# Three places instead of two for layer two's gate and up weights, down weights fetched tile by tile, in a two-layer attention and feed-forward kernel

## The reference, cut to what matters

```python
x = x + _L0_xattn_ref(_layernorm(x), ctx_512, ...)
x = x + _L0_ffn_ref(_layernorm(x), ...)      # a dense gelu part (512 to 2048 to 512) and 8 experts, top 2
x = x + _L1_xattn_ref(_layernorm(x), ctx_512, ctx_512, ...)
x = x + _L1_ffn_ref(_layernorm(x), ...)      # silu(x @ w_gate.T) * (x @ w_up.T), then @ w_down.T
```

## Time and profile before

| | |
|---|---|
| median of 3 runs | 1854.75 us (1850.45 to 1861.82) |
| profiled execution, its own time | 1854.27 us |
| span of the profiled execution | 1852.5 us |
| TensorE busy | 1693.0 us, 91% |
| VectorE busy | 1130.6 us, 61% |
| ScalarE busy | 810.7 us, 44% |
| mean granted TensorE clock | 0.966 |

### The profile page before, as it was taken

The page is one execution under the profiler, slowest core; times in us unless marked ns, Lnnn a source line. Parts: engine busy times, 40 slices in busy tenths (PEclk is TensorE's granted clock), DMA queues, the critical chain, the costliest instruction groups (busy, mean ns, idle before and its releaser), DMA issues.

```text
span 1852.5 us, 27428 instructions
## 1 busy us (share of the span) xinstructions
PE 1693.0 (91%) x9460; PEld 1347.2 (73%) x9460; DVE 1130.6 (61%) x2444; ACT 810.7 (44%) x1799; POOL 267.1 (14%) x301
## 2 busy tenths in 40 slices
PE   3688997999989999888999999889999999999998
PEld 2566776878988887676766766677776678678887
DVE  5777679755665646974677764499556663543222
ACT  3566553234665643322565665323155461422111
POOL 1213234610121203220010100132100000000000
PEclk8689998999999999999999999999999999999999
DMA  3324548798888787879889863687862445245562
GB/s 104 114 92 165 182 164 292 245 358 281 262 284 327 248 289 287 308 258 340 298 261 302 283 221 112 233 292 272 301 208 89 120 137 205 80 144 196 195 215 92
DMA packets 135593, 410.06 MB, mean 221 GB/s; under 512 B 16032, under 2 KB 30752, under 8 KB 131744
## 3 DMA queue, kind: packets, MB, share of 16 engines
q1 hardware_dynamic: 123552, 368.98, 58.1%
q0 software_dynamic: 11904, 39.33, 6.5%
HBM read 303.92 MB, written 104.33 MB: 220 GB/s over the span
## 4 chain that ended last, share of the span: by engine, by line
PE 38%; DVE 5%; DMA 4%; ACT 2%; issue 2%; SPq 0%; ACTq 0%; DVEq 0%
PE ps L1226 10%; PE ps L1228 9%; PE ps L1227 9%; PE ps L1380 4%; PE ps L1389 2%; DMA gu<-w_dram 2%; PE ps L1372 2%; DMA raw<-in_ffn_w 1%; ACT Pr L1605 1%; PE ps L1373 1%; DMA w_dram<-raw 0%; DVE mnb L2008 0%; DVE raw L1737 0%; DVE x L2036 0%; PE ps L1232 0%
## 5 line engine op out<-in xcount | busy, mean ns | idle before, releaser
L1226 PE MATMUL ps<-xT,gu 128*128 128x512 f32 (+1 forms) x1392 | 531.2, 382 | 49.6 <-DMA gu<-w_dram 24.7
L1228 PE MATMUL ps<-xT,gu 128*128 128x512 f32 (+1 forms) x1392 | 512.6, 368 | 0.0
L1227 PE MATMUL ps<-xT,gu 128*128 128x512 f32 (+1 forms) x1392 | 512.2, 368 | 0.0
L1226 PEld LDWEIGHTS ps<-xT,gu 128*128 128x128 f32 x1392 | 269.9, 194 | 96.3 <-issue 46.1
L1228 PEld LDWEIGHTS ps<-xT,gu 128*128 128x128 f32 x1392 | 269.2, 193 | 43.1
L1227 PEld LDWEIGHTS ps<-xT,gu 128*128 128x128 f32 x1392 | 269.7, 194 | 35.5
L1226 PE MATMUL ps<-wd,hid 128*128 128x512 f32 x604 | 248.3, 411 | 28.9 <-issue 14.0
L1227 PE MATMUL ps<-wd,hid 128*128 128x512 f32 x604 | 238.0, 394 | 0.0
L1228 PE MATMUL ps<-wd,hid 128*128 128x512 f32 x604 | 237.9, 394 | 0.0
L1437 ACT ACTIVATE hid<-act 128x512 fp32r<-128x512 f32 (+1 forms) x174 | 99.9, 574 | 289.3 <-DVE act L1717 280.8
L1717 DVE TENSOR_TENSOR act<-act,ps 128x512 f32<-128x512 f32 (+1 forms) x174 | 106.7, 613 | 167.7 <-PE ps L1228 158.4
(11 more groups left out here) (283 smaller groups left out, 2362.4 us busy)
## 6 DMA issues: line engine op xcount, KB each, us to landing
gu<-w_dram SPq DMA_DIRECT2D x192, 512.0 KB
raw<-in_ffn_w SPq DMA_DIRECT2D x78, 768.0 KB
wd<-w_dram SPq DMA_DIRECT2D x96, 512.0 KB, 6.2
w_dram<-raw SPq DMA_DIRECT2D x48, 512.0 KB, 4.6
w_dram<-gu SPq DMA_DIRECT2D x16, 1024.0 KB, 10.2
raw<-in_ffn_w POOLq DMA_DIRECT2D x48, 256.0 KB, 5.3
QT<-q_dram SPq DMA_DIRECT2D x48, 256.0 KB, 5.9
y_dram<-x SPq DMA_DIRECT2D x23, 512.0 KB
```

Source lines behind the costliest of these rows:

```text
L1226: mm(out_ap, ah, bh, start=start, stop=False)
L1227: mm(out_ap, ah, bl, start=False, stop=False)
L1228: return mm(out_ap, al, bh, start=False, stop=stop)
```

## The change

It has three parts.

1. **A third place in layer two.** The space of `acc` is given back at once in the allocation, and a tile `gu_third` of the same size takes it. From the first tile of layer two on (`LAYER2`, s = 110) gate's and up's weights go round three places instead of two, and a load waits for tile s - 3 instead of s - 2. The first tile that uses the third place (F10.2) waits until `acc` of F03 has been stored (`dn_stored`).
2. **Down weights one tile at a time.** The plan holds each `("pre", s, 2)` behind `("pre", s, 1)` of the same tile. This holds in F02 and F03 too.
3. **Early pieces paced.** The plan holds `eload` n behind the start of tile F03.(n // 4), where before it held `eload` 0 alone behind the start of F03.0.

No arithmetic instruction and no byte moved is added or taken away.

```diff
+    LAYER2 = FIRST["F", 1, 0]
+    def gu_slot(s):
+        return (s - LAYER2) % 3 if s >= LAYER2 else s % 2
+    def gu_before(s):
+        return s - 3 if s > LAYER2 + 2 else s - 2 if s < LAYER2 + 2 else None
...
-            on = [("up" if m == 1 else "gate", s - 2)] if m < 2 else [("down", GROUP_OF[s - 6], group_tiles(GROUP_OF[s - 6]) - 1)] if s >= 6 else []
+            on = [("up" if m == 1 else "gate", gu_before(s))] if m < 2 and gu_before(s) is not None else [("dstore", LAST_DOWN["F", 0, 3], TB - 1)] if m < 2 else [("down", GROUP_OF[s - 6], group_tiles(GROUP_OF[s - 6]) - 1)] if s >= 6 else []
...
-        if item == ("eload", 0):
-            return [("gate0", FIRST["F", 0, 3])]
+        if item[0] == "eload":
+            return [("gate0", FIRST["F", 0, 3] + item[1] // 4)]
+        if item[0] == "pre" and item[2] == 2:
+            return [("pre", item[1], 1)]
...
-        acc = sb("acc", [P, TB, D])
+        acc_scope = ExitStack()
+        acc = sb("acc", [P, TB, D], F32, acc_scope)
+        acc_scope.close()
+        gu_third = sb("gu_third", [P, 2, 2, D], F32R)
...
+        def weights_at(s, m):
+            return gu_third[:, m, :, :] if gu_slot(s) == 2 else gu[:, gu_slot(s), m, :, :]
...
                     if m == 0:
-                        sp.wait_ge(gate_done, nth("gate", s - 2))
-                        load(gu[:, s % 2, 0, :, :].bitcast(F32), from_).then_inc(g_loaded[s % 2], 16)
+                        if gu_before(s) is None:
+                            sp.wait_ge(dn_stored, 16 * TB * B)
+                        else:
+                            sp.wait_ge(gate_done, nth("gate", gu_before(s)))
+                        load(weights_at(s, 0).bitcast(F32), from_).then_inc(g_loaded[gu_slot(s)], 16)
```

More of the change, by code:

```diff
@@ L608, in two_layers, with loads_of @@
             PIECE[item] = len(PIECE) + 1
[L610 to L615, removed]
+    def loads_of(tiles, place):
+        return {s: 16 * sum(1 for v in tiles[:n + 1] if place(v) == place(s)) for n, s in enumerate(tiles)}
+    GU_LOADS, WD_LOADS = loads_of(PRE, gu_slot), loads_of(PRE, lambda s: s % 6)
+    GU_STORES, WD_STORES = loads_of(KEPT, gu_slot), loads_of(KEPT, lambda s: s % 3)
     def early_store(n):
@@ L780, in two_layers @@
         w_high, w_low = sems("w_high", "w_low")
-        g_loaded, u_loaded, gu_stored = (sems(n + "0", n + "1") for n in ("gate_loaded", "up_loaded", "gu_stored"))
+        g_loaded, u_loaded = (sems(n + "0", n + "1", n + "2") for n in ("gate_loaded", "up_loaded"))
+        gu_stored = sems("gu_stored0", "gu_stored1")
         wd_loaded, wd_stored = sems(*(f"wd_loaded{n}" for n in range(6))), sems(*(f"wd_stored{n}" for n in range(3)))
@@ L960, in _ @@
                         if is_kept(s - 2):
-                            sp.wait_ge(gu_stored[s % 2], GU_STORES[s - 2])
+                            sp.wait_ge(gu_stored[gu_slot(s)], GU_STORES[s - 2])
                     else:
@@ L966, in _ @@
                     if m == 0:
-                        sp.wait_ge(gate_done, nth("gate", s - 2))
-                        load(gu[:, s % 2, 0, :, :].bitcast(F32), from_).then_inc(g_loaded[s % 2], 16)
-                    elif m == 1:
-                        sp.wait_ge(up_done, nth("up", s - 2))
-                        load(gu[:, s % 2, 1, :, :].bitcast(F32), from_).then_inc(u_loaded[s % 2], 16)
+                        if gu_before(s) is None:
[3 more added lines that the diff above has]
+                        load(weights_at(s, 0).bitcast(F32), from_).then_inc(g_loaded[gu_slot(s)], 16)
+                    elif m == 1:
+                        if gu_before(s) is None:
+                            sp.wait_ge(dn_stored, 16 * TB * B)
+                        else:
+                            sp.wait_ge(up_done, nth("up", gu_before(s)))
+                        load(weights_at(s, 1).bitcast(F32), from_).then_inc(u_loaded[gu_slot(s)], 16)
                     else:
@@ L1236, in quarter @@
                 q, cols = x_slot(s), columns(s)
-                return three(ps[:, gate_bank(s) + m, 0:width(s)], gu[:, s % 2, m, 0, rows(d)], gu[:, s % 2, m, 1, rows(d)],
+                return three(ps[:, gate_bank(s) + m, 0:width(s)], weights_at(s, m)[:, 0, rows(d)], weights_at(s, m)[:, 1, rows(d)],
                              xT[:, q, 0, d, cols], xT[:, q, 1, d, cols], d == 0, d == KD - 1)
@@ L1250, in _ @@
                     else:
-                        pe.wait_ge(g_loaded[s % 2], GU_LOADS[s])
+                        pe.wait_ge(g_loaded[gu_slot(s)], GU_LOADS[s])
                     if what == "E" and h == 0:
@@ L1271, in _ @@
                     else:
-                        pe.wait_ge(u_loaded[s % 2], GU_LOADS[s])
+                        pe.wait_ge(u_loaded[gu_slot(s)], GU_LOADS[s])
                     quarter(1, s, 0)
```

## The result

| | before | after |
|---|---|---|
| median | 1856.0 us of 4 runs (1850.45 to 1861.82) | 1828.03 us of 4 runs (1824.07 to 1835.68) |
| profiled execution, its own time | 1854.27 us | 1828.03 us |
| its span | 1852.5 us | 1826.3 us |

The ratio is 0.9854, with a 95% interval of 0.9809 to 0.9898: 28 us, or 1.5%, faster. The forecast was 1838 us, and the range of 1822 to 1859 holds the result.

The account below looks back on a forecast made before the run. TensorE, busy 1693.0 of 1852.5 us, sets the end; only its idle and low-clock time can be won. Terms 1.0 + 3.0 + 3.7 + 2.0 + 1.4 + 5.3 + 0.6 = 17.0 us, from 1854.75 to 1838; range 1822 to 1859.

Parts of the forecast that it names:

- the account that I held to be the likeliest: Whole kernel: waits for weights go, VectorE and the query loads take back half; 1830 to 1845 us, chance 0.43.
- a different placement of the same steps: Every order after F02.0 may shift in a new plan; worth about 6 us either way, taken as 0.
- F03.3, 3.0 us kept of 9.4: Layer one: down weights leave the queue's front, but full DMA returns the wait later; bounds 0 and 9.4 us, 3.0 kept.
- F10.8 and F10.11, 2.0 us kept of 11.9: Layer two: weight waits go, but VectorE, 91% busy, makes TensorE wait instead; bounds 0 and 11.9 us, 2.0 kept.
- The terms of the other tiles in the stretch: Third place's gains: 3.7 us at F10.7, 1.4 at F10.15, 5.3 of 5.9 at F11.3.
- F02, 1.0 us gain kept: F02's two waits for weights total 1.5 us; the down hold wins 1.0.
- 5.3 us at F11.3: Wait and slow stretch of 5.9 us; 5.3 kept because query loads follow the last step between the layers.
- Its price of 0 at F10.2: F10.2 must wait for the last store of `acc`; cost 1.4 us at most, taken as 0.
- The 10.4 us for low-clock stretches: After long weight waits TensorE ran at its lower clock; the stretches' losses sum to 10.4 us.
- B: All is won, VectorE steps spread over more tiles; up to 35.1 us, 1820 to 1830 us, chance 0.17.
- C: VectorE and DMA take nearly all, waits only change name; 7 us won, 1848 us (1845 to 1854.75), chance 0.25.
- D: F10.7 to F11.2: densely packed steps cost 10 us, slower than before; 1861 us (1855 to 1870), chance 0.15.

Follow-up runs that it names:

- e4: Kernel before plus the hold on down loads and the pace of early pieces, still two places: 1837.35 us, 0.9889.
- e2: Kernel before plus one down load at a time alone, two places everywhere: 1840.14 us, 0.9900.
- e10: Kernel before plus the down hold for F02 and F03 alone, layer two keeping its bursts and two places: 1838.12 us, 0.9914.
- e7: Changed kernel with the down hold only from F03 on, so F02 has its old order: 1844.43 us, 0.9915.
- e1: Changed kernel without the down hold and with the old hold on early pieces, leaving the third place alone: 1853.45 us, 0.9975.
- e6: Changed kernel with the steps between the layers for batches 2 and 3 held behind the start of F10.5: 1837.31 us, 0.9890.
- e8: Changed kernel with three places at run time from F10.6 on, but a plan made as if for two: 1836.71 us, 0.9872.
- e5: Changed kernel without the pace of the early pieces: 1829.16 us, 0.9851.
- e3: Kernel before plus the pace of the early pieces alone: 1854.43 us, 0.9982.
- e9: Kernel before plus the down hold for layer two's tiles alone, two places: 1861.62 us, 1.0038.

## Why the prediction was right, and where it was wrong

**What the whole is made of.** Both holds bring the time to 0.9889 (e4; 0.9900 as e2), nearly all of it by the hold in layer one (e10, 0.9914). The third place adds some 0.3%, the pace nothing. The forecast of 17.0 us had it the other way round: 13.0 us from the third place at F10.7 to F11.7, and 4.0 us from the down loads. That the range of 1822 to 1859 holds 1828 is in part luck: most of the gain came from a part that the sum had at 0, and the result lies outside the 1830 to 1845 of the account that I held to be the likeliest.

**The step that failed** is "So a different placement of the same steps is worth about 6 us either way. I take 0." The new plan was the largest term. e10 changes only the waits in the plan of layer one and moves the kernel by 16 us. I had bounded the value of a placement by one pair of waits in one stretch. F02 fits this bound (6.2 us dearer). But the order in F02 decides when the loads and steps of the next 350 us go out, and the bound says nothing of that.

**F03.3, 3.0 us kept of 9.4.** Undersized. The stretch F03.0 to F10.5 won 10.8 us, above even the upper end. I had reasoned that DMA, at a share of 1.03, would give the wait back at the first scores. With F02's old order that is what happened: e7 waits 6.65 us there for the queries. In the new order `KT` leaves 15.0 us earlier and the attention runs ahead of F03.3, so neither wait exists; a wait of 3.2 us for ScalarE inside the first scores is new. The reasoning held for the order that I looked at, not for the one that came. The wait itself is also unsteady: 7.2 us in the kernel before and 10.9 in e1, which has the same order up to there.

**F10.8 and F10.11, 2.0 us kept of 11.9.** Undersized, by the same cause. With the third place alone the mechanism is there: e1 waits 7.4 us for `hid` behind VectorE's list. But I took 93% for what VectorE manages, and it is at 94.9% from 1223 to 1287; and I held its list to begin where it had begun. It begins 18 us ahead of F10.5 now, and TensorE waits 5.4 us for `x` where it waited 4.7. e6 takes that start away and loses 9 us; as its rows show, the loss did not take the form of a longer wait for VectorE, so how much of the 20.2 us the early start explains is shown only to that 9. And e6 still wins 15.2 us in this stretch with the late start. The terms of the other tiles in the stretch (3.7, 1.4, 5.3) and the 11.9 sum to 22.3 us; 20.2 came.

**F02, 1.0 us gain kept.** Wrong in sign: 6.2 us dearer, with a 6.6 us wait for the copy into `acc`.

**The third place.** Right about what it does (waits for weights in its stretch 14.7 to 0, in e1 too) and about its size in its own stretch (12.7 measured in e1, 12.4 forecast). Wrong in that this stays: 8.3 us came back after F11.5. The prediction kept 5.3 us at F11.3 "because the attention of batches 2 and 3 follows, whose query loads come only after the last of those steps"; this is where it came back, with 4.4 us of waits for `QT`. Its price of 0 at F10.2 was right, though the margin was smaller: from the last store's issue to F10.2's first matmul 8.1 us (1135.5 to 1143.59), not 18.8, and the load itself had 5.6. The 20.2 us for store and load, each taken at 10.1, were far too high; the store landed in 2.4.

**The clock.** The 10.4 us for low-clock stretches were a fair size: in F10.5 to F11.5 TensorE's busy time fell by 6.4 us at 610 matmuls, of the 8.2 us counted there. Over the whole execution the mean granted clock did not rise, 0.966 before and 0.964 after.

**The pace.** Right: the same program.

**The rivals.** The result lies in the span that B had, by another way: B's VectorE work was to go later, and it went earlier. C's claim that waits only change their name is what e1 shows. D's claim, a dense plan that costs 6 us, came true in F02, at layer one's end, and in the next stretch the change won more than that. D's condition, a share of VectorE above 93% behind 1198, was met without its price.

**The signs.** Waits for weights under 5 us: yes, 2.7. Single down issues: mostly; one pair in F02 and one in F03, and from 1173.28 on one pair in each group of four. Two pairs of gate and up issues before a group's down products end: yes, but the kernel before has them too (1228.19 to 1236.37), so this sign tells nothing. VectorE above 93% with longer waits for `x`: 93.2 to 94.9%, waits 0.7 us longer. No wait before F10.2: yes. Loads of early pieces at the same tiles: no, the first three go out in F02.14 instead of F03.0; e2 has the same without the pace, so it is the order's doing. No wait for `QT` of over 5 us: yes. And "a gain or loss in stretches that had no `gu` wait, which would be the new plan's doing" was the sign that spoke: F02's loss.

**A rule weighed.** In 1173 to 1190 us DMA moved 398 GB/s at a share of 1.02, and TensorE was busy 17.00 of 17 us. The Trainium skill ("SBUF — State Buffer", section "A bandwidth-pool intuition that's wrong") gives about 358 GB/s from memory to a core, as its half of what two cores share. This trace is above that figure, as that of before was; the kernel runs on one core, and no run here loads a second. By my reading of the full share as "no more to be had", these 17 us would have cost time, and here they cost none. In the kernel before, 1184 to 1204 at a share of 1.03 ended in the wait of 5.27 us. So in these two traces the share alone does not tell whether TensorE will wait.

## What to carry to other kernels

Where one planner orders everything, a wait added to the plan is an edit of the plan first and of the transfers second: compare the engines' lists before and after, and find the first place where they part, before costing the waits named in the profile. Cut both traces at the same tiles and look for gains where the removed wait was not, and then apply the edit in one half of the program at a time; this split the cause in two runs, which taking the parts of the change one by one had not. Gains of single edits in one stretch do not add up where they win the same idle time (6.3, 12.7 and 13.0 us made 20.2). A removed wait counts only up to the next thing that must arrive: in e1 12.7 us were won and 8.3 of them paid back after it, 4.4 at the queries.

## What the runs showed of the hardware

The changed kernel, e2, e4, e5, e6, e8 and e10, whose lists are the same up to F02.0, began that tile between 677.9 us (e6) and 684.2 us (e8) in their profiled executions. So 6 us of difference, 0.3% of the time, can stand in a trace before anything differs, and a stretch must be compared with that in mind.

The same wait varies from run to run with the order unchanged: before F03.3, 7.2 us in the kernel before, 8.6 in e3, 10.9 in e1 and 6.0 in e9. A single trace gives such a wait to some 5 us, no better.
